# Two slots of a retention network: both gates and both products of u ahead of its roundings and low halves, A's sums of h's halves ahead of f's low halves, Wf1's low half on VectorE

## The reference, cut to what matters

```python
def block(h, p):
    wk, w1, b1, w2, b2, gg, gb, wf1, bf1_, wf2, bf2_, lg, lb = p
    r = _retention(h, wk)                       # causal q k^T, row-normalised, times v
    m = r @ w1 + b1
    a, gate = jnp.split(m, 2, axis=-1)
    m = a * jax.nn.silu(gate) @ w2 + b2         # u = a * silu(gate)
    m = _groupnorm1(m, gg, gb)                  # over all of a sequence
    y = m + h
    f = jax.nn.gelu(y @ wf1 + bf1_, approximate=False) @ wf2 + bf2_
    return (_layernorm(f + y, lg, lb), None)
```

## Time and profile before

| | |
|---|---|
| median of three runs | 2366.42 us (2365.89 to 2367.8) |
| profiled execution, its own time | 2365.91 us |
| its span in the profile | 2364.2 us |
| TensorE busy | 2339.5 us (99%) |
| VectorE / ScalarE / GpSimd busy | 1614.0 / 1332.9 / 1516.3 us |
| granted TensorE clock | 0.996 of full speed |

### The profile page before, as it was taken

How to read it: one execution, slowest core, us unless ns; L and a number is a source line. 1 busy time by engine, 2 the same in 40 slices (tenths; PEclk the granted TensorE clock), 3 DMA queues, 4 the chain that set the end, 5 groups by cost and what they waited for, 6 DMA issues and landing times. The chain is left out here.

```text
span 2364.2 us, 34451 instructions
## 1 busy us (share of the span) xinstructions
PE 2339.5 (99%) x11146; PEld 1953.5 (83%) x11146; DVE 1614.0 (68%) x2938; ACT 1332.9 (56%) x2319; POOL 1516.3 (64%) x1637
## 2 busy tenths in 40 slices
PE   9999999999999999999999999999999999999998
PEld 7888888888888888878888888888888888888886
DVE  3677777777777777878887756665566756574545
ACT  5666766676667666656555544444444444444443
POOL 3476876677667867768888845555555556455544
PEclk9999999999999999999999999999999999999999
DMA  7244454445444453246767656463465454454342
GB/s 258 50 99 107 102 140 112 102 103 139 112 107 107 109 125 103 86 139 205 257 206 221 219 188 215 159 188 144 176 188 179 164 180 154 164 195 168 141 158 76
DMA packets 410545, 357.24 MB, mean 151 GB/s; under 512 B 284944, under 2 KB 373264, under 8 KB 394000
## 3 DMA queue, kind: packets, MB, share of 16 engines
q1 hardware_dynamic: 409408, 354.44, 49.1%
q10 hardware_dynamic: 976, 0.81, 0.1%
HBM read 250.99 MB, written 104.20 MB: 150 GB/s over the span
## 5 line engine op out<-in xcount | busy, mean ns | idle before, releaser
L887 POOL TENSOR_TENSOR hid_lo<-full,hid_hi 128x512 fp32r<-128x512 f32 x384 | 505.6, 1331 | 500.4 <-ACT full L1165 459.2
L1664 DVE SCALAR_TENSOR_TENSOR full<-ps,bias_cols,sum 128x512 f32<-128x512 f32 x384 | 288.1, 750 | 199.6 <-PE ps L1965 182.0
L1963 PE MATMUL ps<-hid_hi,m_w 128*128 128x512 f32 x1024 | 399.5, 390 | 0.1
L1965 PE MATMUL ps<-hid_hi,m_w 128*128 128x512 f32 x1024 | 398.5, 389 | 0.0
L1964 PE MATMUL ps<-hid_lo,m_w 128*128 128x512 f32 x1024 | 398.4, 389 | 0.0
L1162 ACT ACTIVATE hid_hi<-ps,bias_cols 128x512 fp32r<-128x512 f32 x128 | 88.3, 690 | 507.0 <-PE ps L1965 507.0
L1963 PE MATMUL ps<-te_hi,m_w 128*128 128x512 f32 x896 | 351.1, 392 | 3.0 <-DVE sum L1655 1.1
L1965 PE MATMUL ps<-te_hi,m_w 128*128 128x512 f32 x896 | 348.8, 389 | 0.0
L1964 PE MATMUL ps<-te_lo,m_w 128*128 128x512 f32 x896 | 348.6, 389 | 0.0
L1963 PEld LDWEIGHTS ps<-hid_hi,m_w 128*128 128x128 f32 x1024 | 192.2, 188 | 40.5 <-issue 0.5
L1965 PEld LDWEIGHTS ps<-hid_hi,m_w 128*128 128x128 f32 x1024 | 192.2, 188 | 40.4
(11 more groups left out here) (211 smaller groups left out, 5636.1 us busy)
## 6 DMA issues: line engine op xcount, KB each, us to landing
m_w<-prepared SPq DMA_DIRECT2D x96, 1408.0 KB, 6.1
prepared<-m_w SPq DMA_DIRECT2D x32, 1408.0 KB, 5.8
h_store<-h_out SPq DMA_DIRECT2D x32, 512.0 KB, 3.8
we_raw<-in_W SPq DMA_DIRECT2D x64, 256.0 KB, 6.4
gate_bc<-gate_rows SPq DMA_DIRECT2D x64, 256.0 KB, 6.4
z<-z_store SPq DMA_DIRECT2D x30, 512.0 KB, 3.9
hT_store<-turned_h SPq DMA_DIRECT2D x96, 128.0 KB, 3.2
h_in<-h_store SPq DMA_DIRECT2D x24, 512.0 KB, 5.4
```

The source lines that it names most:

```text
L887: nc.gpsimd.tensor_tensor(out=hid_lo[:, k, :], in0=full[:, k, :], in1=f32(hid_hi[:, k, :]), op=ALU.subtract).then_inc(hid_ready, 1)
L1664: nc.vector.scalar_tensor_tensor(out=full[:, k, :], in0=src, scalar=b1_col(e, 2 * fp + BLOCK_ROW[k]), in1=other[:, :], op0=ALU.add, op1=AL ...
L1963: nc.tensor.matmul(out, w[0], x[0], start=first, stop=False, skip_group_check=True)
L1965: return nc.tensor.matmul(out, w[1], x[0], start=False, stop=last, skip_group_check=True)
```

## The change

On ScalarE and VectorE, in both slots: the gate of chunk 1 comes ahead of the rounding of u's chunk 0, and the product of chunk 1 ahead of the low half of chunk 0. On GpSimd, `whole_hT` runs in halves of 256 columns (both slots), and A's stands ahead of `split_f(B)`. At the three seams ScalarE rounds Wf1 right behind f's last rounding, ahead of the table load, and VectorE, not GpSimd, makes its low half, as one instruction of 128x1024 ahead of A's products; GpSimd waits for it before Wf2's.

```diff
@@ GpSimd
                 for c in range(DC):
-                    nc.gpsimd.tensor_tensor(out=y[s][:, c, :], in0=f32(hT_sp[s][0][:, c, :]), in1=f32(hT_sp[s][1][:, c, :]),
-                                            op=ALU.add).then_inc(g_rstd[s], GN_ADD // DC)
+                    for part in (slice(0, S // 2), slice(S // 2, S)):
+                        ins = nc.gpsimd.tensor_tensor(out=y[s][:, c, part], in0=f32(hT_sp[s][0][:, c, part]),
+                                                      in1=f32(hT_sp[s][1][:, c, part]), op=ALU.add)
+                    ins.then_inc(g_rstd[s], GN_ADD // DC)
...
                         layernorm_gain(pool, nc.gpsimd, B_, earlier, z[B_][:, :, :], BLOCKS)
+                    whole_hT(A_, now)
                     split_f(B_, before)
-                    whole_hT(A_, now)
                     layernorm_rstd(A_, before)
...
-                if seam:
-                    split_weight("f1", now.layer)
                 rstd_group(A_, now)
                 if seam:
+                    pool.wait_ge(w_lo, split_count("f1", now.layer))
                     split_weight("f2", now.layer)
@@ ScalarE
                     gate(B_, before, 0)
                     high_h(A_, now)
-                    high_u(B_, before, 0)
                     gate(B_, before, 1)
+                    for c in range(DC):
+                        high_u(B_, before, c)
                     if seam:
                         next_high_weight("vm", now.layer, m_psum[B_], before)
-                    high_u(B_, before, 1)
...
                     high_f(B_, before, FC - 1)
+                    if seam:
+                        next_high_weight("f1", now.layer, f1_psum[B_], before)
...
-                gate(A_, now, 0)
-                high_u(A_, now, 0)
-                gate(A_, now, 1)
-                high_u(A_, now, 1)
+                for c in range(DC):
+                    gate(A_, now, c)
+                for c in range(DC):
+                    high_u(A_, now, c)
...
-                if seam:
-                    next_high_weight("f1", now.layer, f1_psum[B_], before)
                 high_t(B_, now)
@@ VectorE
+            def low_weight(name, follows, l):
+                dve.wait_ge(w_hi, high_count(name, l))
+                dve.wait_ge(w_lo, split_count(follows, l))
+                nc.vector.tensor_tensor(out=wide(1, name), in0=raw[:, SPANS[name]], in1=f32(wide(0, name)),
+                                        op=ALU.subtract).then_inc(w_lo, 1)
...
-                    low_u(B_, before, 0)
                     gated(B_, before, 1)
-                    low_u(B_, before, 1)
+                    for c in range(DC):
+                        low_u(B_, before, c)
...
+                if seam:
+                    low_weight("f1", "m2", now.layer)
                 gated(A_, now, 0)
+                gated(A_, now, 1)
                 low_u(A_, now, 0)
-                gated(A_, now, 1)
                 if before:
                     residual(B_, before, 0)
                 low_u(A_, now, 1)
```

## The result

| | before | after |
|---|---|---|
| median of runs, us | 2367.1 (6 runs, 2365.8 to 2368.1) | 2386.7 (6 runs, 2386.0 to 2389.4) |
| span of the profiled execution, us | 2364.2 | 2384.5 |
| ratio of the times, 95% interval | | 1.0085 [1.0072, 1.0098] |

The change costs 19.6 us by the medians and 20.3 us by the spans; 16.7 us were forecast.

What follows compares the result with a forecast made beforehand. TensorE, busy 99% of the span, was taken to bound the kernel. Ordinary steps +5.3, steps 14 and 15 +4.2 and seams +7.2 gave +16.7 us on 2365.9, forecast 2382.5 us; range 2368 to 2388.

Steps and rivals of the forecast that it cites:

- Sums ahead of f's low halves: GpSimd, `whole_hT(A)` ahead of `split_f(B)`: TensorE waits for f 1.05 us per ordinary step, 2.1 late, 3.9 per seam.
- the rule of gaps: TensorE: a matmul's stall costs its gap + 0.27 us, one for groupnorm's inputs its gap + 0.16.
- A meeting costs 0.45 us, and meetings add: GpSimd's sums beside VectorE's two subtractions of `low_hT(B)`: 0.45 us longer for each, 0.90 together.
- rival 1: Overlaps with VectorE do not add, GpSimd keeps its pace, halving is the only extra: +3 us, 2369; chance 0.20.
- Four pieces cost 2.83 us alone: GpSimd's halved sums, four instructions of 128x256: 2.83 us, 0.3 more than the two whole ones (2.54).
- rival 2: Pieces of GpSimd's sums are cheaper than the gain's, each step some 0.6 us better: +8 us, 2375; chance 0.10.
- rival 3: GpSimd's gain starts earlier, so `split_f` is in time and all 8.6 us are won: 2358; chance 0.08.
- The 8.6 us of gains: TensorE's waits for u's low halves and groupnorm's inputs go: 4.1 us in ordinary steps, 4.5 us at seams.
- those for `gin` are gone: Sign of being right: TensorE's waits for groupnorm's inputs vanish; 3.4 us counted for the three at seams.
- Wf1's subtraction costs 1.0 us at a seam: VectorE's new 128x1024 subtraction, once per seam, falls into GpSimd's `split_f` and lengthens it by 1.0 us.
- Slot B's reordering costs nothing: VectorE's two low halves of u come together behind `gated(B, 1)`: taken as 0, TensorE's first wants stay in place.
- The 6 us kept for the range: Slot B, both low halves of u meeting a halved sum: at most 0.3 + 0.11 us per step over 14 steps.

Runs made afterwards that it cites:

- Experiment 1: Changed kernel with A's sums, still in halves, back behind f's low halves on GpSimd; 2363.4 us, ratio 0.9985 to the kernel before.
- experiment 4: Changed kernel plus one extra 128x512 VectorE subtraction with two SBUF inputs ahead of slot B's first low half of h; 2394.0 us, ratio 1.0115.
- experiment 2: Kernel before with only `whole_hT(A)` moved ahead of `split_f(B)`, sums in whole rows; 2377.3 us, ratio 1.0047.
- experiment 8: Changed kernel with Wf1's low half back on GpSimd and ScalarE's rounding of Wf1 again behind A's roundings of u; 2385.0 us, ratio 1.0077.
- Experiment 5: Changed kernel with VectorE making h's low half by `hT_in` times 0, one SBUF input, instead of the subtraction; 2376.8 us, ratio 1.0041.
- experiments 3 and 6: 3: changed kernel, sums in whole rows, 2391.6 us; 6: kernel before with only the order on u, 2371.7 us, and with halved sums too, 2363.6 us.

## Why the prediction was right

- **Sums ahead of f's low halves**: right in mechanism and size. By the rule of gaps f's stalls are 9 x 1.01 + 2 x 2.5 + 3 x 3.65 = 25.0 us; the prediction's terms, before the gains are taken off, are 9 x 1.05 + 2 x 2.1 + 3 x 3.9 = 25.4. Read from the starts of the matmuls they are 26.4 us. Experiment 1 removes all but 2 us of them. The late steps came out 0.4 us higher each, as `split_f` took 6.51 us there and not 6.04: one meeting more.
- **A meeting costs 0.45 us, and meetings add** (against rival 1): right; 0.46 us for one more in experiment 4.
- **Four pieces cost 2.83 us alone** (against rival 2): right; 2.82 us at the seam, where they meet no subtraction. By the Trainium skill, "GPSIMD Engine Reference", section "Elementwise — side-by-side cycle accounting", an estimated 2.2 us would have come out; the trace disagrees with that.
- **The gain starts earlier** (rival 3): did not happen. In the ordinary step the sums begin 5.84 us ahead of the first matmul on f (217.81, 223.65); by the earlier trace rows the gain ended 223.45 - 217.65 = 5.80 us ahead of it before.
- **The 8.6 us of gains**: right in size; u's waits and slot A's `gin` waits went, and the starts give 8.8 us for them. The reason given is only one of two: experiment 1 shows that the edits on u and Wf1 remove these waits, experiment 2 that the moved sums do it alone. In the changed kernel the edits therefore won nothing, and that the sum is right all the same is luck: each wait can be taken off only once. The sign "those for `gin` are gone" did not hold (below).
- **Wf1's subtraction costs 1.0 us at a seam**: right in place and size; 1.18 - 0.23 = 0.95 us in experiment 8.
- **"Slot B's reordering costs nothing"**: right for this change, and only because of the halves, whose worth the prediction did not see. Without them it costs 8.1 us (2371.7 against 2363.6). The 6 us kept for the range were reckoned for the halved sums, and nothing of them came; with whole rows the same place costs 0.8 us a step, twice the 0.3 + 0.11 allowed.
- **What was missing**: the prediction took 16.7 us, the spans say 20.3. The term that was left out is Wvm's rounding, which the paragraph on what costs nothing does not name. It moves one place back on ScalarE (262.23 in place of 260.01 us), and with it GpSimd's Wvm subtraction and B's sums, which then fall on groupnorm's smallest operations: 3 x (0.50 + 0.16) = 2.0 us of `gin`'s stalls in slot B of the seams. The fourth wait for `gin` (step 14, 0.38 us shown) is new too. There VectorE stood 0.51 us between its last statistics (L1419) and their aggregate (L1423), where in experiment 8's kernel it stood 0.16. That wait is in all six kernels that make Wf1's low half on VectorE and in none of the other five; why an edit at the seams shows in step 14 stays open. By starts these four cost 2.3 us. Another 1.0 us is f's stalls above their terms, 26.4 against 25.4, of which 0.45 us fell into a stretch with a lower clock (last section). Some 0.3 us are left unassigned.

The rule of the Trainium skill, "SBUF — State Buffer", section "Who interferes with whom", agrees with the main rows: both partners are held (2.04 for 1.49 us, 3.73 for 2.83). The subtraction with one input in PSUM, which holds nobody, agrees too. Experiment 5 does not speak against it, although its operation has one SBUF input: the same section lists `tensor_scalar` among the operations that can enter a mode which takes the shared ports, and the trace has it at 0.38 us where the subtraction takes 0.69.

## What to carry to other kernels

An in-order engine's queue has its own deadlines: before a job is moved ahead of another, compare the room in front of the later job's consumer with the moved job's length *beside what will then run on the engine that shares its memory path*. Idle time in front of a deadline is not free: here 1.6 us of GpSimd's idle time was also the time in which VectorE subtracted undisturbed. And gains read from separate waits are not additive with a delay upstream of them: the delay pays for them first.

## What the runs showed of the hardware

- Small operations are held as well: two-element operations on VectorE took 0.66 and 0.57 us beside GpSimd's pieces of 128x256 instead of 0.16 (changed kernel, seam). Halving GpSimd's instructions shortens what others wait: two 128x512 subtractions took 3.10 us beside instructions of 128x512 (experiments 3 and 6) and 2.00 beside those of 128x256 (changed kernel).
- The granted clock is not the same in every stretch. In the changed kernel, right behind the longest stall of the seam in step 8 (1.18 us), it was 0.57 from 541 to 545 us, and matmuls started 0.43 us apart instead of 0.23; that seam cost 0.45 us more than the other two. In experiment 4's kernel it was 0.50 (1.2 GHz) from 545 to 550 us at the same place and 0.83 from 926 to 936, and 1.5 and 1.3 us were lost there.
- Not every execution starts at the same pace. TensorE's first eight matmuls with the weights to be folded, in the changed kernel and in that of experiment 8:

```profile
6.21 1.99 PE L2002 MATMUL ps<-fold_kqv,fold_kqv 128*128 128x256 f32 x8 [0.86 <-DMA fold_kqv<-in_WkqvT]
```

```profile
6.20 3.78 PE L2001 MATMUL ps<-fold_kqv,fold_kqv 128*128 128x256 f32 x8 [0.85 <-DMA fold_kqv<-in_WkqvT]
```

  The code is the same and the granted clock is recorded as 1.00 (2.4 GHz) in both, yet the second takes 1.8 us longer, and the whole layer part is shifted by 2.0 us. Each of the eleven kernels was profiled once, and six of these executions were of the second kind. What decides it was not found; where two kernels differ by a few microseconds, a profiled span alone can mislead by that much.
